# Two bursts of small matmuls a unit, split loads, and a new order of opening and tail in a two-layer attention and FFN kernel

## What is computed

```
x = x + L0_xattn(layernorm(x), ctx, ctx, mask, Wq, Wk, Wv, Wo)
x = x + L0_ffn(layernorm(x), A, B, Wr)
x = x + L1_xattn(layernorm(x), ctx, Wq, Wk, Wv, Wo)
x = x + L1_ffn(layernorm(x), W, bias, A, Bf, coeffs, scales)
```

```
q = apply_rope((query @ Wq).reshape(b, 64, 32, 128))
k = apply_rope((key @ Wk).reshape(b, 64, 8, 128))
v = (value @ Wv).reshape(b, 64, 8, 128)
logits = 30 * tanh(einsum(q, k) * 0.0883883 / 30)       # 4 query heads to a kv head
weights = softmax(where(mask, logits, -1e30))
attn = einsum(weights, v).reshape(b, 64, 32 * 128) @ Wo
```

## Times and profile before

| what | us |
|---|---|
| median of 3 runs | 944.78 (944.35 to 945.8) |
| the profiled execution's own time | 945.55 |
| its span, first to last instruction | 943.7 |
| TensorE busy | 887.4 |
| mean granted TensorE clock | 0.975 of 2.4 GHz |

### The profile page before, as it was taken

How to read it: one execution, slowest core, us unless ns; L and a number is a source line. 1 busy time by engine, 2 the same in 40 slices (tenths; PEclk the granted TensorE clock), 3 DMA queues, 4 the chain that set the end, 5 groups by cost and what they waited for, 6 DMA issues and landing times.

```text
span 943.7 us, 12573 instructions
## 1 busy us (share of the span) xinstructions
PE 887.4 (94%) x4762; PEld 703.6 (75%) x4762; DVE 498.1 (53%) x908; ACT 359.1 (38%) x843; POOL 305.1 (32%) x248
## 2 busy tenths in 40 slices
PE   5586999999999999999999987999999999999998
PEld 4464777777777777777777765768988888888776
DVE  6645456555645655655565643645124544554684
ACT  4251122132123123123122222336667676666642
POOL 4164235355345256146255442100002121112132
PEclk9798999999999999999999998889999999999999
DMA  8011012102102202111120132000002110120002
GB/s 278 29 56 46 13 45 91 50 30 90 57 3 88 68 27 75 57 60 31 57 79 26 37 109 78 18 16 12 13 11 58 34 45 19 63 76 1 1 1 90
DMA packets 27517, 48.03 MB, mean 51 GB/s; under 512 B 4225, under 2 KB 5377, under 8 KB 27329
## 3 DMA queue, kind: packets, MB, share of 16 engines
q1 hardware_dynamic: 27456, 47.23, 15.3%
HBM read 44.98 MB, written 2.23 MB: 50 GB/s over the span
## 4 chain that ended last, share of the span: by engine, by line
PE 78%; ACT 8%; DVE 7%; issue 3%; DMA 3%; POOL 1%; SPq 1%; POOLq 0%; DVEq 0%; ACTq 0%
PE PB L1046 21%; PE PB L1047 19%; PE PB L1048 19%; PE PB L1202 5%; PE PB L1132 3%; PE PB L1107 3%; PE PB L1053 2%; ACT Eb L797 2%; PE PB L1217 2%; PE PB L1234 2%; ACT Oh L673 1%; DVE Ol L1017 1%; PE PB L1117 1%; ACT qb L787 1%; DVE sm L999 1%
## 5 line engine op out<-in xcount | busy, mean ns | idle before, releaser
L634 POOL TENSOR_TENSOR qb<-qb,arena 128x512 f32<-128x512 f32 x64 | 82.5, 1288 | 199.3 <-DVE arena L902 199.2
L673 ACT ACTIVATE Oh<-PB 128x512 fp32r<-128x512 f32 (+2 forms) x160 | 70.8, 463 | 194.7 <-PE PB L1132 176.7
L829 DVE TENSOR_TENSOR xs<-xs,PB 128x512 f32<-128x512 f32 x112 | 76.6, 685 | 77.1 <-PE PB L1048 74.2
L1046 PE MATMUL PB<-WOh,Oh 128*128 128x512 f32 x256 | 105.7, 413 | 1.4 <-DVE Ol L935 1.4
L1048 PE MATMUL PB<-WOh,Ol 128*128 128x512 f32 x256 | 100.4, 392 | 0.0
L1047 PE MATMUL PB<-WOl,Oh 128*128 128x512 f32 x256 | 100.4, 392 | 0.0
L899 DVE TENSOR_TENSOR qb<-PB,ropeq 128x512 f32<-128x512 f32 x64 | 44.0, 688 | 100.8 <-PE PB L1048 100.8
L1046 PE MATMUL PB<-xTh,WQh 128*128 128x512 f32 x192 | 80.2, 418 | 0.4 <-DVE xTl L876 0.4
L1047 PE MATMUL PB<-xTl,WQh 128*128 128x512 f32 x192 | 76.8, 400 | 0.0
L1048 PE MATMUL PB<-xTh,WQl 128*128 128x512 f32 x192 | 75.9, 395 | 0.0
L625 POOL TENSOR_TENSOR WQl<-stage,WQh 128x512 fp32r<-128x512 f32 x36 | 46.1, 1285 | 81.0 <-ACT WQh L673 71.9
(11 more groups left out here) (195 smaller groups left out, 2079.5 us busy)
## 6 DMA issues: line engine op xcount, KB each, us to landing
stage<-in_wq SPq DMA_DIRECT2D x44, 256.0 KB, 3.2
stage<-in_wo SPq DMA_DIRECT2D x44, 256.0 KB, 2.9
arena<-recs SPq DMA_DIRECT2D x64, 128.0 KB, 2.9
stage<-in_wk SPq DMA_DIRECT2D x14, 256.0 KB, 3.6
arena<-in_ctxT SPq DMA_DIRECT2D x8, 256.0 KB, 4.4
xs<-in_x SPq DMA_DIRECT2D x8, 256.0 KB, 5.5
stage<-in_wv SPq DMA_DIRECT2D x8, 256.0 KB, 4.8
out<-xs SPq DMA_DIRECT2D x8, 256.0 KB, 2.2
```

What stands on the lines that cost most here:

```text
L634: e.tensor_tensor(dst, dst, tmp, ALU.add).then_inc(s_radd)
L673: return e.activation(dst, src, ACT.Copy)
L829: e.tensor_tensor(xs[:, i, :], xs[:, i, :], PB[b][:, :], ALU.add).then_inc(free[b])
L1046: e.matmul(dst, Ah, Bh, start=(k == 0), stop=False)
```

## The change

`plan()` has a new order, and a few helpers follow it.

- In a unit the small groups stand in two bursts: `b0(u,0)`, `sum0(u-1,1)`, `d0(u-1,0)` and later `b0(u,1)`, `sum0(u,0)`, `d0(u-1,1)`. The chain of a unit now ends in the next unit. `norm0` of a half stands between output projections.
- A `load` step is apart from its `split` step: the load of split n+3 is issued right behind split n, and the first ones are placed by hand in the opening.
- The opening: mask, rope and identity are loaded from ScalarE's DMA queue, the `keep` copy and GpSimd's constants come first, the second half of the context is loaded early, queries q0 start before the statistics of HI are taken, and the splits of wq0 lie between the transposes.
- The first layer norm keeps its intermediate numbers in PSUM (`mvP`, `lnP`), and its formula uses two-input operations with one operand in PSUM. GpSimd passes that point only after the twelve operations.
- The order at the end of the first layer: two keys tiles in the last unit, statistics before the last chain, other splits and other homes for `wk1`; `k1(2,0,*)` and `v1(0,0..2)` between the FFN's steps. `e0` waits for each wo0 low part by itself.

```diff
--- before.py
+++ after.py
@@ -114,44 +114,50 @@
...
+    step("load", "wk0", 0)
+    step("consts")
+    step("ctx_load", 0)
+    for c in range(2):
+        step("load", "wv0", 0, c)
+    for i in LO:
+        step("x", i)
+    step("ctx_load", 1)
+    step("load", "wq0", 0)
     split("wk0", 0)
     step("ctx", 0)
-    for i in LO:
-        step("x", i)
     for c in range(2):
         split("wv0", 0, c)
-    step("ident")
-    step("rope_table")
+    for i in HI:
+        step("x", i)
     for i in LO:
...
     step("rstd", 0, 0)
-    for n in range(4):
-        split("wq0", n)
+    ring.remove(3)
     stage("k0", 0, 0)
-    normed(0, LO, [None, lambda: stage("v0", 0, 3)], [lambda i=i: stage("v0", 0, i) for i in range(3)])
-    for i in range(4):
+    normed(0, LO, [lambda: split("wq0", 1), lambda: (step("v0_move", 0, 0), stage("v0", 0, 3)),
+                       lambda: (step("v0_move", 0, 1), split("wq0", 2))],
+           [lambda i=i: stage("v0", 0, i) for i in range(3)] + [lambda: split("wq0", 0)])
+    tile("many", bank=3)
+    step("mask_tables")
+    step("ctx", 1)
+    for i in range(2, 4):
         step("v0_move", 0, i)
-    step("ctx", 1)
-    for i in HI:
-        step("x", i)
-    step("mask")
+    q0(0, 0)
+    split("wq0", 3)
     for i in HI:
         step("stats", 0, i)
+    q0(0, 1)
     step("rstd", 0, 4)
-    tile("many", bank=3)
-    step("mask_tables")
-    for n in range(4):
-        q0(0, n)
+    q0(0, 2)
+    q0(0, 3)
     stage("k0", 0, 1)
...
-    for b in (2, 3, 4, 5):
+    for b in (2, 4, 5):
         ring.remove(b)
...
         split("wv0", 1, c)
-    for n in range(4):
-        split("wo0", n)
     for u in range(NU):
@@ -165,26 +171,30 @@
...
         b0(u, 0)
+        if u:
+            sum0(u - 1, 1)
+            d0(u - 1, 0)
         queries(0)
+        queries(1)
+        outputs(0)
+        if u:
+            norm0(u - 1, 1)
+        outputs(1)
+        b0(u, 1)
+        sum0(u, 0)
+        if u:
+            d0(u - 1, 1)
+        queries(2)
+        queries(3)
         if u == NU - 1:
             k1(0, 0, 0)
-        b0(u, 1)
-        queries(1)
-        sum0(u, 0)
-        outputs(0)
-        sum0(u, 1)
-        outputs(1)
+            k1(0, 0, 1)
         norm0(u, 0)
-        queries(2)
-        norm0(u, 1)
-        queries(3)
-        d0(u, 0)
         outputs(2)
         outputs(3)
-        if u and u % 2 == 0:
+        if u % 2 == 0:
             for n in range(4):
                 split("wo0", 2 * u + n)
-        d0(u, 1)
         j, hf = u // 2 + 1, u % 2
@@ -202,12 +212,26 @@
...
         if u == NU - 2:
-            split("wq1", 0, 0)
-            split("wq1", 0, 1)
-            split("wq1", 0, 2)
+            split("wk1", 1, 0)
+            split("wk1", 2, 0)
             split("wv1", 2)
-        if u == NU - 1:
-            step("ffn_load")
+    for i in LO:
+        step("stats", 1, i)
+    step("rstd", 1, 0)
+    sum0(NU - 1, 1)
+    d0(NU - 1, 0)
+    step("ffn_load")
+    k1(1, 0, 0)
+    e0(NU - 1, 0)
+    norm0(NU - 1, 1)
+    e0(NU - 1, 1)
+    d0(NU - 1, 1)
+    k1(1, 0, 1)
+    e0(NU - 1, 2)
+    e0(NU - 1, 3)
+    split("wq1", 0, 0)
+    split("wv1", 3)
@@ -237,30 +261,25 @@
...
-    for i in LO:
-        step("stats", 1, i)
-    step("rstd", 1, 0)
     ring[0:0] = [4, 5]
-    for c in range(4):
-        e0(NU - 1, c)
     for i in HI:
...
     step("rstd", 1, 4)
-    ffn_mid(0, [lambda: split("wk1", 1, 0)], [lambda: k1(0, 0, 1)])
-    split("wk1", 2, 0)
-    split("wv1", 3)
+    ffn_mid(0, [], [lambda: k1(2, 0, 0)])
     ffn_gates(0)
-    ffn_mid(1, [lambda: k1(1, 0, 0)])
+    ffn_mid(1, [], [lambda: k1(2, 0, 1)])
+    split("wq1", 0, 1)
+    split("wq1", 0, 2)
+    split("wk1", 0, 1)
     ffn_gates(1)
-    ffn_delta(0, [lambda: k1(1, 0, 1)])
+    ffn_delta(0, [lambda: v1(0, 0)])
     for i in LO:
...
     step("rstd", 2, 0)
-    k1(2, 0, 0)
-    ffn_delta(1, [lambda: k1(2, 0, 1)])
-    split("wk1", 0, 1)
+    v1(0, 1)
+    ffn_delta(1, [lambda: v1(0, 2)])
     ring[0:0] = [2, 3]
-    normed(2, LO, [lambda i=i: v1(0, i) for i in range(4)])
+    normed(2, LO, [lambda: v1(0, 3)])
     for i in HI:
@@ -340,6 +359,17 @@
...
         stage("dense", i)
+    weights = [st for st in p.steps if st[0] == "split"]
+    ordered = []
+    for st in p.steps:
+        ordered.append(st)
+        if st[0] == "split":
+            n = weights.index(st) + 3
+            if 4 <= n < len(weights):
+                ordered.append(("load", *weights[n][1:]))
+    p.steps = ordered
     return p
...
-        wk_home = [(WKh[:, :], WKl[:, :]), (WOh[:, 1, :], WOl[:, 1, :])]
-        wk1_at = {(0, 0): 0, (1, 0): 1, (2, 0): 0, (0, 1): 0, (1, 1): 0, (2, 1): 0}
+        wk_home = [(WKh[:, :], WKl[:, :])] + wq_home[0:2]
+        wk1_at = {(0, 0): 0, (1, 0): 1, (2, 0): 2, (0, 1): 0, (1, 1): 0, (2, 1): 0}
         wv1_home = [(WVh[:, 0:384], WVl[:, 0:384]), (WVh[:, 512:896], WVl[:, 512:896]),
@@ -553,13 +586,13 @@
...
             for kind, *k in steps:
-                if kind == "split":
+                if kind == "load":
                     n = splits[tuple(k)]
...
                     e.dma_start(staged[:, n % 4, 0:cols], src).then_inc(s_stage[n % 4], 16)
-                elif kind == "ctx":
+                elif kind == "ctx_load":
                     h, = k
...
                         pool.wait_ge(s_one, 3 + r)
+                elif kind == "rstd":
+                    if k == [0, 0]:
+                        pool.wait_ge(s_ln, 12)
                 elif kind == "b0":
@@ -673,7 +703,11 @@
...
             for kind, *k in steps:
-                if kind == "split":
+                if kind == "consts":
+                    e.dma_start(mask32[:, :], a["mask"]).then_inc(s_mask, 16)
+                    e.dma_start(rope[:, :, :], a["rope"].rearrange("p (a n) -> p a n", a=2)).then_inc(s_rope, 16)
+                    e.dma_start(ident[:, :], a["ident"]).then_inc(s_ident, 16)
+                elif kind == "split":
                     n = splits[tuple(k)]
@@ -846,27 +883,29 @@
...
                     dve.wait_ge(s_st, n + 1)
-                    e.bn_aggr(mv[:, i, :], st6[:, i, :]).then_inc(s_st)
+                    e.bn_aggr((mv if ph else mvP)[:, i, :], st6[:, i, :]).then_inc(s_st)
                 elif kind == "rstd":
...
                     r = slice(i0, i0 + 4)
-                    v, y, b, c, nm = (lnb[:, m, r] for m in range(5))
+                    y, nm = lnb[:, 1, r], lnb[:, 4, r]
+                    v, b, c = ((lnb if ph else lnP)[:, m, r] for m in (0, 2, 3))
+                    mean, var = ((mv if ph else mvP)[:, r, m] for m in range(2))
                     dve.wait_ge(s_st, 2 * (8 * ph + i0 + 4))
...
                         dve.wait_ge(*xn_done(ph - 1, i0 + 3))
-                    e.tensor_scalar(v, mv[:, r, 1], EPS, None, ALU.add).then_inc(s_ln)
+                    e.tensor_scalar(v, var, EPS, -0.5, ALU.add, ALU.mult).then_inc(s_ln)
                     dve.wait_ge(s_ln, n + 1)
-                    e.tensor_scalar(y.bitcast(i32), v.bitcast(i32), -0.5, 1597463007.0, ALU.mult, ALU.add).then_inc(s_ln)
+                    e.tensor_scalar(y.bitcast(i32), v.bitcast(i32), -0.5, 519526879.0, ALU.mult, ALU.add).then_inc(s_ln)
                     for g in range(3):
                         dve.wait_ge(s_ln, n + 3 * g + 2)
-                        e.scalar_tensor_tensor(b, y, -0.5, y, ALU.mult, ALU.mult).then_inc(s_ln)
+                        e.tensor_tensor(b, v, y, ALU.mult).then_inc(s_ln)
                         dve.wait_ge(s_ln, n + 3 * g + 3)
-                        e.tensor_tensor(c, b, v, ALU.mult).then_inc(s_ln)
+                        e.tensor_tensor(c, b, y, ALU.mult).then_inc(s_ln)
                         dve.wait_ge(s_ln, n + 3 * g + 4)
...
                     dve.wait_ge(s_ln, n + 11)
-                    e.scalar_tensor_tensor(nm, mv[:, r, 0], -1.0, y, ALU.mult, ALU.mult).then_inc(s_ln)
+                    e.scalar_tensor_tensor(nm, mean, -1.0, y, ALU.mult, ALU.mult).then_inc(s_ln)
                 elif kind == "xsplit":
```

23 lines of the change are left out of this document (10 added, 13 removed).

## The result

The changed kernel took 913.81 us (median of 4 runs, 912.45 to 914.12) against 944.66 us of the kernel before (4 runs, 944.35 to 945.8). The ratio is 0.9668, with a 95% interval of 0.9652 to 0.9685. The forecast was 909, with 898 to 921 as its range. The profiled execution of the changed kernel has a span of 912.3 us, that of the kernel before 943.7: 31.4 us less, where the sum said 35.2.

What follows compares the result with a forecast made beforehand. TensorE, busy 94% of the span, was taken as the bound, with idle time and slow clock mainly in the opening and from 550. 943.7 - 32.2 - 11.4 + 0.4 + 8 = 908.5, given as 909 us by the median, range 898 to 921.

Steps and rivals of the forecast that it cites:

- Opening: Start to first scores: first q0 at 23.4 instead of 36.2, gain 12.8 us; first scores at 47.4.
- VectorE's thin cover of 24 us: First q0 to first scores: kept at 24 us; five ropes just in time, scores up to 4 us late otherwise.
- Unit 0: First unit: 20.2 us instead of 39.45, with waits covered and small groups moved out; unit 1 starts at 67.6.
- Bursts: Units 1 to 13: six separate small groups become two bursts, saving 0.88 us a unit, -11.4 us; bounds 0 and 17.
- The chain over two units: Within units: reciprocal, trip and normalization need about 7.5 us, leaving 6 us of slack, so no wait.
- rival 4: Units: reciprocals' trip waits on SyncE behind loads, d0 waits for it; 951 with 3 us of wait a unit; chance 0.03.
- The last unit and the FFN: End of first layer: new waits, covered waits and moved work sum to +8 us, bounds -4 and +14.
- From q1 on: From the first q1 to the end: same steps, order and buffers, so 0 us.
- The tail fits: Last unit and FFN: hand-placed key and value products cover the waits, +8 becomes about -2, 899; chance 0.2.
- Bursts win nothing: Units: switches inside a burst cost as much as those to large matmuls, 920; chance 0.15 shared with another rival.
- the opening is queue-bound: Opening: late x or wq0 loads, or failing VectorE cover, cost 4 to 8 us, 915; chance 0.15.
- not as it says: Split loads don't come earlier because SyncE sits before a chain wait; only the opening is won, 921; chance 0.15, shared.

Runs made afterwards that it cites:

- e2b_sbuf_no_wait: Changed kernel with first-layer statistics and Newton chain in SBUF instead of PSUM and without GpSimd's wait for the chain, step order kept: 914.38 us.
- e3_splits_early: Changed kernel with the four wq0 splits back ahead of the normalization, statistics and chain in SBUF, no GpSimd wait: 919.97 us.
- e2_tables_late: Changed kernel with keep copy and mask tables back behind context, statistics and Newton chain of the second half on VectorE: 923.14 us.
- e1b_apart_no_wait: Changed kernel with bursts taken apart by large products, two-unit chain kept, values groups placed further back so none should wait: 927.27 us.
- e1_apart: Changed kernel with a large product between any two small groups in units 1 to 14, two-unit chain kept: 958.67 us.
- e5_wk_late: Changed kernel with three splits (two key weights, one value weight of the second layer) moved behind unit 15's small groups on ScalarE: 908.55 us.
- e6_stats_late: Changed kernel with statistics and Newton chain of the first four tiles moved behind the values of unit 15 on VectorE: 907.30 us.
- e7_splits_past_gates: Changed kernel with three weight splits (two of wq1, one of wk1) moved behind the second half's gates and first delta products: 907.95 us.
- e10_value_ahead: Changed kernel with three moves (key/value splits, statistics, splits behind gates), one keys product ahead of e0(14,0), one value product ahead of first q1: 886.52 us.
- e4_load_at_split: Changed kernel with each weight load from the fifth on issued at its own split instead of three splits ahead: 916.65 us.

## Why the prediction was right, and where not

- **What bounds the kernel.** Right. Units were bound by TensorE's own instructions; only the bursts moved them.
- **Opening.** First query product forecast at 23.4, measured 23.63; first scores 47.4 and 46.83; unit 1 at 67.6 and 66.74. The chain took 2.4 us for 2.3. It began 1.1 us later than forecast (13.39 for 12.3) and ScalarE then took 7.0 us for 7.4, so two errors cancel in part, and by the spread of first scores above an agreement within 1 us says little. The reason given for it (GpSimd's wait, the splits behind) was right only in the order of the steps: the wait itself and PSUM are worth nothing there (e2b_sbuf_no_wait), and splits left ahead would have cost their 5 us through ScalarE's queue, not through the chain (e3_splits_early). The table's place is worth 8.6 us (e2_tables_late).
- **VectorE's thin cover of 24 us.** It held: 23.2 us from the first q0 to the first scores.
- **Unit 0.** Forecast 20.2 us, measured 19.91, from 39.45. That it had been waiting is shown by the rows above, but no run tests it.
- **Bursts.** 0.22 for each separate group and nothing between neighbours: measured 0.88 us a unit, 33.65 less 32.77, and 0.87 when undone (e1b_apart_no_wait). The estimate from the Trainium skill, TensorEngine Tiling (Array Packing), section Key Properties, was 0.78. The units fit the neighbours' value. Between the small groups, which have three modes, the rows leave nothing for a drain: 1.01, 0.36 and 1.06 us are their lengths alone. At the border to large products 0.22 us are lost, but there the number type changes too (fp32 and fp32r), and no run here tells the two apart. The kernel before has a hint: four fp32 transposes on the whole array, between products in fp32r, lose nothing ahead of them (55.81 to 55.93, the usual 0.12) but 0.09 behind them (56.28 to 56.49), so part of the loss needs no other tiling mode. The neighbours' row was the better ground.
- **The chain over two units.** No wait, as forecast, but the slack was taken too large. The prediction gave 7.5 us to the chain and found 6 us of slack. In a unit of the changed kernel, the sums of half 1 and their normalization stand in these rows, and the values group that wants it is the one at 278.29 in the burst above:

```profile
264.39 0.42 PE L1154 MATMUL PB<-Eb,ones 128*32 128x128 f32 x8
...
274.98 0.68 DVE L964 TENSOR_TENSOR Eb<-Eb,arena 128x512 f32<-128x512 f32 x1
```

  The chain ends at 275.66, 11.3 us after the sums, since two ropes and an addition stand ahead of the normalization on VectorE. 2.6 us are left. A chain that ends too late was nearer than the chance of 0.03 for rival 4 says: e1_apart fell into one by moving a values group and ended 1.4% above the kernel before. The cause that rival 4 gives, a trip that waits behind loads on SyncE, was not at work in it: the trip starts at 252.43, right behind the reciprocal's end at 252.40. The rope ahead of the reciprocal and the nearer user did it.
- **The last unit and the FFN.** Here the sum failed: +8 forecast, +11.1 measured. Its two named waits were nearly right: 7.9 forecast and 8.95 measured ahead of e0(14,0), 4.2 and 4.11 ahead of e0(15,0), and each had the cause it was given (e5_wk_late, e6_stats_late). The one ahead of q1 was 1.82 and 1.13 in two pieces, together the 3 that were said. What the sum left out is the third wait, 2.57 us ahead of the delta products, and the half clock behind it: 5.8 us (e7_splits_past_gates). The prediction gave the three splits that were moved ahead of the gates no term at all: it followed the in-order queues, but not which VectorE work those splits would now run beside. The row for it was there, in the earlier trace rows, a small operation that took 1.20 us beside GpSimd, and it was used for the opening alone. Something came the other way: the kernel before ran at half clock in a stretch of its FFN,

```profile
605.21 1.11 PE L1153 MATMUL PB<-qb,pTb 128*128 128x68 f32 x8 [1.03 <-ACT pTb L673]
...
610.00:620.00 10.00, 7.03 (x24) 6.03 (x25) 2.95 (x17) 3.51 (x7) 2.22 (x2) 0.50 0.17 54
```

  The clock fell at 607.7, ahead of the wait of 2.97 us, which began at 612.34, and behind waits of 1.03 and 0.16 us at 605.21 and 606.92; it came back at 621.4. The twelve matmuls of a keys product in it took 5.3 us (616.05 to 621.31), where those of another took 2.8 (600.33 to 603.14). The changed kernel has this part of its FFN (575 to 590) at full clock. The sum had counted the wait of 2.97 us, not the clock.
- **From q1 on.** 0 forecast, +1.6 measured: nine of the first q1's matmuls at half clock, behind the 1.82 us wait. e10_value_ahead took both away.
- **Loads apart.** They were given no term of their own, and the runs show no need for one (e4_load_at_split).
- **The rivals.** "The tail fits" (899) was not what this change does, but three moves in the order bring it there and below (893.6). "Bursts win nothing" and "the opening is queue-bound" are out by the rows above, and so is "not as it says": the opening alone was not all that was won, and loads that do not come earlier cost nothing that e4_load_at_split can tell.

## What to carry over

Small matmuls of other shapes between large ones cost by the number of borders to the large ones; put them side by side, and check that the chain behind each still ends ahead of its user by what stands on the other queues, not by its own length. When a weight split or any other GpSimd work is moved, look at which VectorE operations will run beside it and who waits for them. A wait on TensorE is to be priced together with the half clock that can follow it: removing waits of 4.11, 2.57 and 1.82 us brought 6.3, 5.8 and 3.3 us here.

## What the hardware showed beside it

- A wait of 2.57 us ahead of eight small matmuls of 64 rows was followed by the lower level of the granted clock for some 10 us (0.53 from 597 to 604, back at 607.7), while two waits of 1.03 and 1.05 us in the 21 us before left it at 1.00. In the kernel before, waits of 1.03 and 0.16 us, 1.7 us apart, were followed by the lower level within 1 us (0.87 from 607 to 608, 0.50 from there on): short waits do not exclude it. The wait of 1.82 us ahead of q1, with 1.13 us shortly before, was also followed by the lower level.
- VectorE operations of 0.22 and 0.16 us became 1.31 and 1.16 us beside one GpSimd operation. The second is a TENSOR_SCALAR with a single input in SBUF. The Trainium skill, SBUF — State Buffer, section Who interferes with whom, names `tensor_scalar` among the operations that can take the port shared with GpSimd, beside those with two SBUF inputs; the pair of rows at 35.94 and 35.76 agrees, and a PSUM source freed it. The prediction left this exception out when it told the rule. The statistics, with one input, took 0.66 to 0.69 us beside GpSimd and apart from it, as that section of the Trainium skill has it.
- The first scores came at 44.66 us (e1_apart) to 47.95 us (e10_value_ahead) in executions of kernels whose opening has the same steps, and the granted clock between 20 and 30 us was 1.00 in the first and 0.66 in the second. A difference of 3 us between the openings of single profiles says nothing here.
